# AdaLN block with attention and a mixture of experts: loop instructions re-spread, last value product by token halves, epsilon and relus on other engines, output order at both ends of the experts

## The chip, the cores and the metric

The kernel runs on one core of a Trainium2 chip. The metric is the device time of one execution in microseconds, the median of three runs. The core has a matrix engine (TensorE, PE in the profile), VectorE (DVE), ScalarE (ACT) and GpSimd (POOL), and SyncE (SP), which only issues transfers here. Each runs its own queue of instructions in order, and they wait for each other on semaphores that the kernel sets by hand.

## The reference, cut to what matters

Eight batches of 512 tokens of width 128 go through two layers:

```python
h = layernorm(x) * (1 + ca) + sa                # ca, sa, ga, cb, sb, gb come from silu(c) @ wmod
q, k, v = einsum('bsx,xAnh->Abnsh', h, w)       # 16 heads of 64
q = q + q_bias
a = q @ k.T / 8 + relative_causal(q @ emb.T / 8)
x = x + ga * (softmax(mask(a)) @ v @ out_kernel + out_bias)
h = layernorm(x) * (1 + cb) + sb
score = softmax(h @ Wg + bg); gate = max(score); idx = argmax(score)
# expert e takes its first 256 tokens in order, others give 0
y = relu(buf @ W1[e] + b1[e]) @ W2[e] + b2[e]   # 16 experts, hidden 512
x = x + gb * y[idx, pos] * gate
```

## The kernel before

Layouts put features on partitions for the projections and tokens on partitions for the softmax. To keep float32 accuracy with the fast matrix format, an operand is split in a high part, rounded by a copy on ScalarE (`vhi`, `qhi`, `khi`, `ohi`, `w1hi`, `xhi`), and a low part, the difference (`vlo`, `qlo`, `klo`, `olo`, `w1lo`, `xlo`); a product is then three products: high by high, low by high, high by low. The relative term is folded into the scores: 64 more rows of the contraction hold sines and cosines, so that one score product gives both terms.

**The attention loop** has 64 steps `j`, one for each pair of heads `a` (0 to 7) of each batch `b`. Each step has eight slots `k`; slot `k` makes the scores of head `k // 4` for one block of 128 queries, longest row first (512, 384, 256, 128 keys). Each engine's `step` function writes its order out by hand. On TensorE (L988 on) a slot issues `scores(j, k)` (L878, L875 for the block of 128), and between the slots the transposes of the probabilities of step j-1 (L888, slots 0 to 5, six groups), the value projection for a later step (L864, slot 1), the output product of step j-2 (L915, slot 2), the query projection of head 0 of step j+1 (L843, slot 4, behind the scores), the key projection of step j+1 (L843, slot 5), the product of probabilities and values of step j-1 (L908, slot 7), and behind slot 7 the query projection of head 1. Two banks of PSUM take the scores in turn, so scores `k` wait for the reduction `k-2`.

VectorE reduces each score block with mask and maximum (L1257), makes `qx` from the projected queries (`evac_q`, L1274), the low parts `klo` (`low_k`, L1280) and `olo` (L1286), one group of transposed probabilities in slot 0 (L1265) and the reciprocals of the sums. In slot 4 the order is: reduction, reciprocal, `evac_q` of head 0. ScalarE takes the exponent of each block (`exps`, L623), copies five of the six transposed groups (`evac_pt`, L632; group 4 behind the exponent of slot 4, group 5 before that of slot 5), and makes the high parts. GpSimd makes `qlo` (L451) and divides the probabilities by the sums (L458, four pieces a head).

Around this, two chains per batch are spread over the slots by `before_attention` (statistics, normalisation, `vhi` and `vlo` of the next batch) and `after_attention` (residual, second layer norm, gate logits, choice of the expert, place in the expert's buffer, for the batch before). For the latter TensorE has extra work in given slots: `turn_a` (L923) at step 1, `logits_t` (L944) at step 3 slot 5, `turn_l` (L951) at step 4, `places` (L963 on) at step 5. GpSimd scatters the finished rows (first-layer output, normalised row, gate times its factor, token number) into a buffer in HBM, `xbuf`, sorted by expert.

**Between loop and experts** there is only the last batch. `weighted` (L908) makes the last value product into one bank, `evac_o` and `low_o` split it, `project_out` (L915) adds it to the output, `residual` (L1295) forms the new x in `h2T`, `turn_a_halves` (L931) transposes it for the statistics (L1176), GpSimd adds epsilon (L372) and takes the power -0.5 (L374), and normalisation, gating and placing follow on small tiles. `fill_in` (L1068) issues products whose result nobody reads.

**The experts** go two tiles of 128 slots at a time. For expert `e`: the input, transposed by TensorE (`turn_e`, L1121; for the first three, a sum of the rows already in `xbuf` and a one-hot product for the last batch, L1088 to L1106), is split by ScalarE (`high_x`, L759) and VectorE (`low_x`, L1597); `hidden` (L1130) makes four tiles of 128 hidden units; relu of tiles 0 to 2 is on ScalarE (L768), of tile 3 on VectorE (L1603); `down` (L1143) makes the output; `output` on VectorE adds the bias, multiplies with the gate and adds x (L1618 to L1621); GpSimd scatters the rows to the result (L513). VectorE also makes the low weights (`low_w1`, L1574). Up to expert 9 the output of expert e-1 is made in round e, then two in one round, from then on that of expert e. SP loads rows of the experts (L286 all columns, L297 the columns behind the first 128 for the first three) and weights (L278, L282); `down` of expert e waits until the output e-2 is written.

## Time and profile before

| | |
|---|---|
| median of 3 runs | 883.32 us (882.67 to 883.62) |
| the profiled execution | 884.27 us |
| span from its first to its last instruction | 882.5 us |
| mean granted TensorE clock | 0.995 |
| busy share of the span: TensorE, VectorE, ScalarE, GpSimd | 98%, 75%, 81%, 60% |
| share of the chain that ended last: TensorE, VectorE | 88%, 2% |

The share of busy time is a mean over stages. The loop ends near 788 us, the experts start near 812, and the last scatter is issued near 874. Matmuls overlap, so the duration of one in a row is longer than the distance to the next; what one costs in a stream is read from the distance of the starts.

### The profile page before, as it was taken

What the parts mean: (1) busy time and instruction counts of PE and PEld (TensorE: products, weight loads), DVE (VectorE), ACT (ScalarE), POOL (GpSimd) and SP (SyncE); (2) the same over time, 40 slices, a digit from 0 to 9 for tenths busy, and PEclk for the clock granted to TensorE, in tenths of its full rate; (3) what the DMA queues carried; (4) which work ended last, traced back from release to release, by engine and by line L of the source; (5) the groups of instructions that cost most, each with busy time, mean ns of one, the idle gap of its engine ahead of it and who ended that gap; (6) DMA issues with size and microseconds to landing.
All of it is one profiled execution on the core that took longest, in us unless ns stands there. A gap on an engine that the chain in (4) does not pass through costs nothing.

```text
span 882.5 us, 17635 instructions
## 1 busy us (share of the span) xinstructions
PE 862.1 (98%) x5579; PEld 687.6 (78%) x5579; DVE 664.7 (75%) x2054; ACT 716.4 (81%) x1996; POOL 532.6 (60%) x796
## 2 busy tenths in 40 slices
PE   8999999999999999999999999999999999999995
PEld 7778877778877778777787777787777877777994
DVE  5878777787878687776878677877778677866684
ACT  5888888888888888888988888888888888874562
POOL 3655566576566765676566765676656646673364
PEclk9999999999999999999999999999999999999998
DMA  8000970000000000000000000000000000015870
GB/s 290 2 1 1 259 197 13 13 19 19 13 13 2 36 1 13 13 19 18 13 13 12 16 13 13 1 21 1 14 13 12 11 13 13 2 34 188 282 225 23
DMA packets 25469, 41.42 MB, mean 47 GB/s; under 512 B 3318, under 2 KB 17511, under 8 KB 24992
## 3 DMA queue, kind: packets, MB, share of 16 engines
q1 hardware_dynamic: 21728, 33.60, 12.6%
q0 software_dynamic: 3072, 5.94, 1.9%
q8 instruction: 45, 0.74, 0.4%
q10 hardware_dynamic: 576, 0.75, 0.3%
q14 instruction: 48, 0.39, 0.1%
HBM read 25.93 MB, written 16.82 MB: 48 GB/s over the span
## 4 chain that ended last, share of the span: by engine, by line
PE 88%; DVE 2%; POOL 1%; DMA 1%; issue 1%; ACT 0%; SPq 0%; POOLq 0%; DVEq 0%
PE bank L878 22%; PE bank L843 16%; PE bank L908 16%; PE bank L888 15%; PE bank L915 5%; PE bank L864 4%; PE bank L875 3%; PE bank L1143 2%; PE bank L1130 2%; DMA x<-xbuf 1%; POOL prob L458 0%; ACT prob L623 0%; PE bank L923 0%; POOL out L513 0%; PE bank L826 0%
## 5 line engine op out<-in xcount | busy, mean ns | idle before, releaser
L458 POOL TENSOR_SCALAR prob<-prob,rsum 128x128 f32<-128x128 f32 (+3 forms) x512 | 263.9, 533 | 220.6 <-DVE rsum L1269 214.9
L623 ACT ACTIVATE prob<-srow,nmax 128x512 f32<-128x512 f32 (+3 forms) x512 | 286.5, 561 | 64.5 <-DVE nmax L1257 61.3
L1257 DVE CUSTOM_DVE_ANT_0 srow<-bank,consts 128x512 f32<-128x512 f32 (+3 forms) x512 | 247.5, 488 | 85.8 <-issue 63.9
L888 PE MATMUL bank<-consts,prob 128*128 128x128 f32 x1280 | 201.9, 272 | 0.2 <-POOL prob L458 0.2
L888 PEld LDWEIGHTS bank<-consts,prob 128*128 128x128 f32 x1280 | 158.2, 141 | 22.8 <-POOL prob L458 0.5
L451 POOL TENSOR_TENSOR qlo<-qx,qhi 128x384 fp32r<-128x384 f32 x128 | 129.2, 1009 | 49.6 <-ACT qhi L588 48.6
L632 ACT ACTIVATE pt<-bank 128x384 f32<-128x384 f32 x318 | 152.3, 496 | 1.4 <-PE bank L888 1.3
L908 PE MATMUL bank<-pt,v 128*64 128x512 f32 (+3 forms) x1024 | 152.0, 439 | 0.3 <-issue 0.2
L878 PE MATMUL bank<-khi,qhi 128*128 128x512 f32 (+2 forms) x384 | 145.7, 380 | 2.7 <-DVE nmax L1257 1.9
L1274 DVE SCALAR_TENSOR_TENSOR qx<-bank,qbias,consts 128x512 f32<-128x512 f32 x128 | 94.2, 736 | 60.9 <-PE bank L843 60.8
L878 PE MATMUL bank<-khi,qlo 128*128 128x512 f32 (+2 forms) x384 | 130.0, 339 | 0.0
L878 PE MATMUL bank<-klo,qhi 128*128 128x512 f32 (+2 forms) x384 | 129.1, 336 | 0.0
L908 PEld LDWEIGHTS bank<-pt,v 128*64 128x64 f32 x1024 | 68.2, 136 | 76.7 <-issue 59.2
L1280 DVE SCALAR_TENSOR_TENSOR klo<-bank,khi 64x512 fp32r<-64x512 f32 x128 | 87.8, 686 | 18.1 <-ACT kx L583 16.1
L588 ACT ACTIVATE qhi<-qx 128x384 fp32r<-128x384 f32 x128 | 66.7, 521 | 38.8 <-DVE qx L1274 38.1
L623 ACT ACTIVATION_READ_ACCUMULATOR prob<-srow,nmax 128x1 f32 x512 | 97.8, 191 | 0.0
L878 PEld LDWEIGHTS bank<-khi,qhi 128*128 128x128 f32 x384 | 72.4, 189 | 16.9 <-issue 5.9
L843 PE MATMUL bank<-hhi,whi 128*128 128x512 f32 x177 | 81.6, 461 | 0.0
L878 PEld LDWEIGHTS bank<-klo,qhi 128*128 128x128 f32 x384 | 72.8, 190 | 7.6
L582 ACT ACTIVATE khi<-bank 64x512 fp32r<-64x512 f32 x128 | 75.3, 588 | 2.0 <-PE bank L843 0.5
L878 PEld LDWEIGHTS bank<-khi,qlo 128*128 128x128 f32 x384 | 72.2, 188 | 5.5
L843 PE MATMUL bank<-hlo,whi 128*128 128x512 f32 x177 | 70.0, 395 | 0.0
(210 smaller groups left out, 1419.5 us busy)
## 6 DMA issues: line engine op xcount, KB each, us to landing
xbuf<-fill SPq DMA_DIRECT2D x4, 1540.0 KB, 23.4
x<-xbuf SPq DMA_DIRECT2D x13, 385.0 KB, 3.5
raw<-in_w SPq DMA_DIRECT2D x16, 256.0 KB, 8.7
prob<-in_w SPq DMA_DIRECT2D x16, 256.0 KB, 4.7
h2T<-in_xt SPq DMA_DIRECT2D x8, 256.0 KB, 2.7
out<-row SPq DMA_DIRECT2D x8, 256.0 KB, 2.3
x<-in_x SPq DMA_DIRECT2D x1, 1792.0 KB, 13.4
modb<-mod_rows SPq DMA_DIRECT2D x1, 1536.0 KB, 8.9
```

Of the source, the lines that this page charges most:

```text
L451: gp.tensor_tensor(qlo[:, h, :], qx[:, h, P:S], qhi[:, h, :], ALU.subtract).then_inc(s["ql"], 1)
L458: end = gp.tensor_scalar(part, part, rsum[:, par, 4 * h + q:4 * h + q + 1], 1.0, ALU.mult, ALU.mult)
L582: act.activation(khi[0:HD, h, :], prb[0][h * HD:(h + 1) * HD, :], ACT.Copy, scale=C_QKV)
L623: act.activation(prob[:, par, h, QOFF[q]:QOFF[q] + P * (q + 1)], srow[:, k % 4, 0:P * (q + 1)], ACT.Exp, bias=nmax[:, par, k:k + 1], scale ...
L632: act.activation(pt[:, h, KOFF[g]:KOFF[g] + GW[g]], source[:, 0:GW[g]], ACT.Copy)\
L843: last = pe.matmul(out, w[:, a, cols], h, start=(i == 0), stop=(i == 2))
L878: last = pe.matmul(out, a[:, h, (q - 1) * P:q * P], b[:, h, 0:P * (q + 1)], start=(i == 0), stop=(i == 2))
L888: last = pe.transpose(out[:, n * P:(n + 1) * P], prob[:, par, h, QOFF[q] + k * P:QOFF[q] + (k + 1) * P], ident)
L908: last = pe.matmul(otb[h * HD:(h + 1) * HD, k * P:S], v[:, g, k, at + h * HD:at + (h + 1) * HD], pt[:, h, KOFF[k]:KOFF[k] + S - k * P], st ...
L1257: dve.tensor_tensor_reduce(out=srow[:, k % 4, 0:w], in0=scb[k % 2][:, 0:w], in1=mask[:, S - w:S], scale=-1.0, scalar=BIG, op0=ALU.add, op1 ...
L1274: dve.scalar_tensor_tensor(qx[:, h, :], prb[h][:, :], qbias[:, h, a:a + 1], qtab, ALU.add, ALU.mult).then_inc(s["qe"], 1)
L1280: dve.scalar_tensor_tensor(klo[0:HD, h, :], prb[0][h * HD:(h + 1) * HD, :], C_QKV, khi[0:HD, h, :], ALU.mult, ALU.subtract).then_inc(s["kl ...
```

## The change

It moves instructions and waits, and in two places splits one in two.

- In a step, TensorE projects head 0's queries of step j+1 ahead of score product 4 instead of behind it (not in the first and the last step of the loop), VectorE makes `qx` of it ahead of the reduction of slot 4, and ScalarE copies group 4 ahead of the exponent of slot 4.
- `low` (vlo of the next batch) goes from VectorE, step 4 slot 7, to GpSimd, step 4, ahead of the first division.
- `logits_t` goes from step 3 slot 5 to slot 7, its copy from slot 6 to slot 7. `limits` loses the token numbers, which go to step 3 slot 5, and moves from step 5 slot 3 to slot 5.
- Epsilon of the first batch's first norm and of the last batch's second is added on VectorE.
- The last value product, its split, the last output product and the last residual are done by halves of the tokens in two banks.
- The first hidden layer orders its twelve products so that those with `xhi` come first. All four relus are on ScalarE. The outputs of expert 14 are written by halves in round 15's place, its second half in bank 0. SP issues the other columns of the first experts before the rows of experts 3 and 4.

```diff
 SP
             for e in range(EARLY, NSLOT):
+                other_columns(e - EARLY)
                 rows(e)
-                other_columns(e - EARLY)
 GpSimd
-            def root(i, n):
-                waits(gp, ("pch", 1), (f"rst{i + 1}", n))
-                gp.tensor_scalar(vare[:, i, :], mom[:, i, :, 1], EPS, None, ALU.add).then_inc(s[f"va{i + 1}"], 1)
+            def root(i, n, added=False):
+                gp.wait_ge(s["pch"], 1)
+                if not added:
+                    gp.wait_ge(s[f"rst{i + 1}"], n)
+                    gp.tensor_scalar(vare[:, i, :], mom[:, i, :, 1], EPS, None, ALU.add).then_inc(s[f"va{i + 1}"], 1)
...
+            def low(n):
+                gp.wait_ge(s["vhi"], n + 1)
+                gp.tensor_tensor(vlo[:, :], hn[:, :], vhi[:, :], ALU.subtract).then_inc(s["vlo"], 1)
...
+                    if not last and a == 4:
+                        low(b + 1)
                     divide(j, a % 2, 0)
...
-            root(1, B)
+            root(1, B, True)
 ScalarE
-                    if before and k == 5:
-                        evac_pt(j - 1, 5)
+                    if before and k in (4, 5):
+                        evac_pt(j - 1, k)
                     exps(j, par, k)
...
-                    if before and 2 <= k < 5:
+                    if before and k in (2, 3):
                         evac_pt(j - 1, k)
...
-            evac_o(NJ - 1)
+            for i in range(2):
+                half = slice(i * S // 2, (i + 1) * S // 2)
+                act.wait_ge(s["pv"], NJ + i)
+                act.activation(ohi[:, half], half_o[i][:, half], ACT.Copy, scale=C_QKV * C_OUT).then_inc(s["oe"], 1)
...
-                    for n in range(NB - 1):
+                    for n in range(NB):
                         act.wait_ge(s["hm"], NB * e + n + 1)
 TensorE
                 for k in range(8):
+                    if k == 4 and a == 3 and first:
+                        pe.wait_ge(s["whi"], 8)
+                        pe.wait_ge(s["wlo"], 4)
+                        pe.wait_ge(s["wlo_k"], 2)
+                    if k == 4 and before and after:
+                        project_q(j + 1, n, m, 0)
                     scores(j, k)
...
-                    if (a, k) in ((1, 5), (3, 5), (4, 4), (5, 4)) and not first:
+                    if (a, k) in ((1, 5), (3, 7), (4, 4), (5, 4)) and not first:
...
-            weighted(NJ - 1, PAIRS - 1, NJ, 3)
-            fill_in(6)
-            project_out(NJ - 1, PAIRS - 1)
...
+            for i in range(2):
+                for k in range(2 * i + 2):
+                    c0_, c1_ = max(k * P, i * S // 2), (i + 1) * S // 2
+                    for h in range(2):
+                        at = (PAIRS - 1) % 4 * P + h * HD
+                        last = pe.matmul(half_o[i][h * HD:(h + 1) * HD, c0_:c1_],
+                                         v[:, (PAIRS - 1) // 4, k, at:at + HD],
+                                         pt[:, h, KOFF[k] + c0_ - k * P:KOFF[k] + c1_ - k * P],
+                                         start=(k == 0), stop=(k == 2 * i + 1))
+                last.then_inc(s["pv"], 1)
             fill_in(4)
+            for i in range(2):
+                half = slice(i * S // 2, (i + 1) * S // 2)
+                pe.wait_ge(s["ol"], NJ + i)
+                for n, (w, o) in enumerate(((wohi, ohi), (wohi, olo), (wolo, ohi))):
+                    end = pe.matmul(opb[:, half], w[:, PAIRS - 1, :], o[:, half], start=False, stop=(i == 1 and n == 2))
+            end.then_inc(s["op"], 1)
+            fill_in(2)
             turn_a_halves()
...
+            def hidden_first():
+                pe.wait_ge(s["w1l"], 1)
+                pe.wait_ge(s["xt"], 1)
+                for n in range(NB):
+                    for i, w in enumerate((w1hi, w1lo)):
+                        pe.matmul(bank[2 + n][:, 0:CAP], w[:, 0, n, :], xhi[:, 0, :], start=(i == 0), stop=False)
+                pe.wait_ge(s["xl"], 1)
+                for n in range(NB):
+                    pe.matmul(bank[2 + n][:, 0:CAP], w1hi[:, 0, n, :], xlo[:, 0, :], start=False, stop=True)\
+                        .then_inc(s["hm"], 1)
 VectorE
                 for k in range(8):
+                    if k == 4 and before and after:
+                        evac_q(j + 1, (a + 1) % PAIRS, 0)
                     scores(j, par, k)
...
-                if (a, k) == (4, 7):
-                    low(n)
-                if (a, k) == (3, 6):
+                if (a, k) == (3, 5):
+                    token_numbers(b)
+                if (a, k) == (3, 7):
                     logits_out(b)
...
-                if (a, k) == (5, 3):
-                    limits(b)
                 if (a, k) == (5, 5):
                     place(b)
+                    limits(b)
...
             aggregate(1, B)
+            add_eps(1, B)
...
-                relu(e, e % 2)
...
-                if e >= LAGGING:
+                if LAGGING <= e < E - 2:
                     output(e)
-            relu(E - 1, 1)
+            for t in range(ST):
+                output(E - 2, t, t + 1)
             for t in range(ST):
                 output(E - 1, t, t + 1)
```

## Rows read from the trace of the kernel before

**Rows 1.** Windows, one batch: length, busy time by engine, clock, DMA share, GB/s

```profile
175.40:272.50 97.10, 97.03 (x610) 76.21 (x610) 75.39 (x237) 83.84 (x237) 62.07 (x95) 1.00 0.04 15
```

**Rows 2.** Timeline of TensorE, a step: start us, us, engine, line, operation, count

```profile
204.12 0.47 PE L878 MATMUL bank<-khi,qhi 128*128 128x512 f32 x1
...
204.90 0.40 PE L843 MATMUL bank<-hhi,whi 128*128 128x512 f32 x1
...
205.59 0.49 PE L888 MATMUL bank<-consts,prob 128*128 128x128 f32 x3
```

**Rows 3.** Timeline of VectorE and ScalarE, the same step

```profile
205.19 0.69 DVE L1257 CUSTOM_DVE_ANT_0 srow<-bank,consts 128x512 f32<-128x512 f32 x1 [0.90 <-issue]
...
206.65 0.85 ACT L632 ACTIVATE pt<-bank 128x384 f32<-128x384 f32 x2
```

**Rows 4.** Timeline, end of step 4, step 5, and step 0 of the next batch

```profile
173.80 0.68 DVE L1206 TENSOR_TENSOR vlo<-hn,vhi 128x512 fp32r<-128x512 f32 x1
...
175.18 0.47 PE L878 MATMUL bank<-khi,qhi 128*128 128x512 f32 x1
...
180.29 1.04 POOL L436 TENSOR_TENSOR row<-rsm,modb 128x512 f32<-128x512 f32 x1 [1.37 <-DVE rsm L1362]
...
180.33 1.03 DVE L1376 TENSOR_SCALAR rsm<-rsm 128x4 f32<-128x4 f32 x1
...
183.03 0.50 PE L843 MATMUL bank<-hhi,whi 128*128 128x512 f32 x1
...
218.61 0.50 PE L843 MATMUL bank<-hhi,whi 128*128 128x512 f32 x1
```

**Rows 5.** Timeline of ScalarE and TensorE, a step 2

```profile
243.82 0.49 ACT L632 ACTIVATE pt<-bank 128x384 f32<-128x384 f32 x1
...
244.60 2.38 PE L908 MATMUL bank<-pt,v 128*64 128x512 f32 x16
```

**Rows 6.** Timeline of TensorE, logits of step 3

```profile
255.15 0.43 PE L944 MATMUL bank<-h2T,wgc 128*32 128x128 f32 x8
```

**Rows 7.** Timeline of GpSimd, step 4

```profile
264.08 1.19 POOL L418 TENSOR_TENSOR row<-row,modb 128x512 f32<-128x512 f32 x1
```

**Rows 8.** Timeline of TensorE, first and last batch, fifth score product

```profile
59.22 0.47 PE L878 MATMUL bank<-khi,qhi 128*128 128x512 f32 x1 [0.69 <-DVE nmax L1257]
...
774.01 0.47 PE L878 MATMUL bank<-khi,qhi 128*128 128x512 f32 x1
```

**Rows 9.** Timeline, between the loop and the experts

```profile
800.01 0.75 DVE L1295 SCALAR_TENSOR_TENSOR h2T<-bank,modT,h2T 128x512 f32<-128x512 f32 x1 [0.56 <-PE bank L915]
...
802.75 0.54 POOL L372 TENSOR_SCALAR vare<-mom 128x4 f32<-128x4 f32 x1 [9.65 <-DVE mom L1181]
...
803.37 1.04 POOL L374 TENSOR_TENSOR rstd<-vare,mhalf 128x4 f32<-128x4 f32 x1
...
811.47 0.42 DVE L1597 TENSOR_TENSOR hlo<-bank,hhi 128x256 fp32r<-128x256 f32 x1 [1.11 <-ACT hhi L759]
```

**Rows 10.** DMA issues at 817 (KB, us to landing), timeline of the experts

```profile
x<-xbuf SPq DMA_DIRECT2D x1, 385.0 KB, 3.2
x<-xbuf SPq DMA_DIRECT2D x1, 257.0 KB, 5.0
...
812.04 0.36 PE L1130 MATMUL bank<-hhi,whi 128*128 128x256 f32 x1 [0.33 <-DVE hlo L1597]
...
822.32 0.17 DVE L1615 CAST yidx<-x 128x2 uint32<-128x2 f32 x1 [2.22 <-DMA x<-xbuf]
...
823.86 2.38 PE L1143 MATMUL bank<-prob,srow 128*128 128x128 f32 x16 [1.21 <-DVE row L1621]
...
853.16 1.38 PE L1143 MATMUL bank<-prob,srow 128*128 128x128 f32 x10 [0.62 <-DVE srow L1603]
...
871.67 0.29 DVE L1618 TENSOR_TENSOR xh<-bank,v 128x128 f32<-128x128 f32 x1
...
874.40 0.97 POOL L513 DMA_INDIRECT out<-xh,yidx  x1 [0.30 <-issue]
```

## Prediction of the time after the change

> **What bounds the kernel now.** I read the table of windows first. One batch of attention (64 steps in all, 8 to a batch) takes 97.10 us, TensorE is busy in 97.03 of them at a granted clock of 1.00, which is the 2.4 GHz level, while VectorE, ScalarE and GpSimd rest for 14 to 35 us [rows 1]. So in the loop an edit is worth what it takes out of TensorE's stream, and the other engines matter only where their lateness opens a hole in it. "Busy" hides small holes, since the ends of matmuls are modelled; I found them by comparing start times in the timeline of TensorE: three products of 512 columns follow each other every 0.23 us, and the first behind fp32 transposes costs 0.08 more (204.12 to 204.90 is 0.78) [rows 2]. Measured against that, three holes recur in each batch [rows 4]. Behind the loop the chain alternates between engines, and there the waits at the ends of rows are the prices [rows 8, 9].
>
> **The loop, part by part.** Nothing is added to or taken from TensorE's work in a step; things change places.
>
> Low half of the next batch's activations (`low`), from VectorE to GpSimd. The 0.68 us at 173.80 stands directly before the low half of the keys, and the next step's first score product starts at 175.18, some 0.22 late [rows 4]. The instruction leaves VectorE, so this hole goes: six batches have it, 6 x 0.22 = 1.3 us. On GpSimd a 128x512 operation of two inputs took 1.19 us [rows 7]; it sits in step 4 behind two of those, before the division. The division of the first head must wait for VectorE's reciprocal anyway, and by the timeline it would be ready about 0.5 us later than now, so GpSimd ends at nearly the same time as that reciprocal. Cover: GpSimd's wait. Without it the 1.2 us would push the low half of the queries that the next step's first score needs, up to 0.5 us per batch. I take 0.
>
> Key projection of step 5. It waits for VectorE's qx, which in step 5 comes behind `limits`: 1.03 us at 180.33 for 512 numbers, ending with the GpSimd operation at 180.29 [rows 4]. TensorE's projection at 183.03 starts 0.21 late; in step 0 the same thing happens behind statistics, 0.095 late at 218.61 [rows 4]. Now the projection of the first head's queries goes ahead of score product 4, and qx ahead of that score's reduction, and `limits` and the token numbers leave the place. qx is then ready about 0.7 us sooner, more than either hole: 7 x 0.21 + 7 x 0.095 = 2.1 us. The projection's new wait, for the low half of the keys, ends some 0.6 us before TensorE gets there.
>
> What this swap makes late. The score's reduction, at 205.19 now, follows a product that ends 0.7 us later; the exponent behind it moves by as much. ScalarE fills part of it by copying transposed group 4 first (that group starts at 205.59 on TensorE in either order). The two copies, now one at 206.65 and ending at 207.50 [rows 3], would end about 0.33 later, at 207.83. The weighted product needs them at 208.14 (the start of the same product is at 244.60 in the step below), so an ordinary step has 0.2 us left after the hop between engines. Cost 0. In step 2 ScalarE has a 0.77 us normalisation between the two: the last copy ran from 243.82 to 244.31, the product started at 244.60 [rows 5]; 0.25 later plus a hop of 0.1 is a hole of about 0.07. Seven batches: 0.5 us lost. Bounds 0 and 7 x 0.3 = 2.1.
>
> Transposed logits from slot 5 to slot 7 of step 3. They are eight short matmul records of width 32 from 255.15 to 255.50 [rows 6]. In front of them and behind them TensorE pauses about 0.23 each, and again about 0.24 between the full-width and the 64-wide product of slot 7. Placed there, one of the three changes of width is shared. If a change from 32 to 64 costs what the others do, 0.17 us per batch, 1.2 in all; bounds 0 and 1.2; I take 1.0. SP loads the next transposed input only behind these logits, so that load starts 2 us later; it is wanted in the next batch, some 50 us on. The Trainium skill (TensorEngine Tiling (Array Packing), the section with the rule that mode switching requires a drain) says that changing the tiling mode empties the engine. The pauses at 255.15 agree. By that rule one drain per batch goes, by a reading in which they belong to the logits alone none would.
>
> Ends of the loop. At 59.22 the fifth score of a step of the first batch waited 0.87 us in total (0.69 of it shown) for a late reduction [rows 8]; the projection now fills half of it: 0.4. In the last batch no values are projected, TensorE runs ahead, and the fifth score product waits 0.31 us (start at 774.01) [rows 8]; in two of three such steps the projection now goes in: 0.6. Epsilon on VectorE at the very start saves one hop, 0.15 (bounds 0, 0.35).
> Loop and start: 1.3 + 2.1 - 0.5 + 1.0 + 0.4 + 0.6 + 0.15 = 5.05 us.
>
> **The stretch between loop and experts.** The last value product is made by token halves (384 and 896 of the 1280 columns, so the same total). ScalarE's copy and VectorE's low part of the first half lie beside the second half's product; of the second half only half-wide ones stay on the path. A VectorE operation took 0.75 at 512 columns and 0.42 at 256 [rows 9], so the two save about 0.25 + 0.3, the output product's last part and its shorter end 0.3; the residual in two halves costs 0.15 more, and the first half's transposes and statistics run beside the second: 0.15. Sum 0.85 (bounds 0.4 and 1.3). Epsilon: GpSimd's addition at 802.75 took 0.54, the root started at 803.37, 0.62 after it [rows 9]. On VectorE such a 4-column operation comes without the first hop: 0.4 saved. GpSimd is idle there (9.65 us), and the 0.66 us low part of a weight stands behind the addition in VectorE's order. The Trainium skill (SBUF — State Buffer, "SBUF: two separate sides") says that VectorE in a two-port mode and GpSimd lock each other out for a whole instruction. The pair at 180.29 and 180.33 agrees; the rule speaks against more such operations on VectorE while GpSimd works, and by it `limits`, now beside the divisions, can wait for one of their pieces. That delays a reduction with over a microsecond of slack and leaves the sum as it is. Together 1.25 us; what follows up to the first expert moves with it.
>
> **The experts.** The first hidden layer may start before xlo: 812.04 shows 0.33 of waiting [rows 10], worth up to 0.45. I give it 0, since the chain is then held by a transfer (next).
> Order of loads: rows of expert 3 (385 KB) are issued first and land 3.2 us later, the other columns of expert 0 (257 KB) second, 5.0 us [rows 10]. VectorE waits 2.22 us for the latter until 822.32; its output frees TensorE at 823.86, and the relu on VectorE behind it stretches that product further, until about 826.0. Swapped, the columns land near 819.9 and the output is ready at about 821.4, before TensorE wants it (822.5). Expert 3's rows now come second, near 822.2, and TensorE wants them at 822.3 or a little sooner: the new end of the wait. The second product then runs 822.55 to 824.25. Gain 1.75 us; bounds 0.45 (only the relu part) and 2.1.
> Expert 10: two outputs in a row on VectorE held its relu, TensorE waited to 853.16 (0.62 shown, 0.89 in the spacing of the experts) [rows 10]. Four relus on ScalarE take this away; but the low part of the next input still stands behind both outputs and comes 0.14 late: 0.75 gained. In an ordinary expert ScalarE's queue has 2.6 of 3.43 us filled, and the low part is ready 0.15 before TensorE asks for it: nothing.
> End: four scatters follow each other at 1.27 us on GpSimd, the last at 874.40, while the first half of the last expert's rows is written at 871.7 [rows 10]. With expert 14 written by halves its two scatters go about a microsecond sooner and no longer hold up expert 15's. Those then start behind their own data, the first 0.9 after it (the hop from VectorE to a scatter in the timeline), the last 1.27 later, near 873.9: 0.5 gained (bounds 0, 0.6).
> Experts: 3.0 us.
>
> **Sum.** 5.05 + 1.25 + 3.0 = 9.3 us. The profiled execution took 884.27 us around a span of 882.5, so this one would take 875.0. It lies 0.95 above the median of the runs, 883.32; from that the forecast is **874.0 us**.
>
> **Rivals.**
> A. The holes of the loop move instead of going: a later reduction or copy (step 2, the root of step 2 on GpSimd before the low queries) takes back what the three holes give. For it: slacks of 0.1 to 0.3 us; against it: each is still positive by rows. The loop then gives about 1.5 instead of 5: 877.6.
> B. The swapped transfers do not help, since the rows of expert 3 land late, and the halves gain nothing because of more instructions: the tail gives 1.7 instead of 4.25: 876.6.
> C. Slower. ScalarE decides: its copy of group 5 ends past the time of the weighted product in every step. It happens from 0.2 us more than I count; at 0.4 us more each of some 55 steps loses 0.2, 11 us, against gains of 9.3: 885.0. For it: ScalarE's queue is unbroken from 203.4 to 211.4 in a step; against it: it then rests 0.8 us, so the lateness doesn't add up from step to step.
> D. It doesn't do what it says: score product 4 is so late that TensorE itself waits and nothing is won in the loop, and the tail is as in B: 881.5.
>
> **Chances.** Forecast 0.60, A 0.20, B 0.12, C 0.04, D 0.04. A measurement here tells 0.2%, 1.8 us, from no change. All but C and part of D are faster: faster 0.94, same 0.02, slower 0.04. Range: the forecast's own bounds are 871.5 to 876; A and B reach to 878.5. I give 871.5 to 878.5.
>
> **What would show it.** Right: a batch of 96.4 or 96.5 us instead of 97.1; VectorE's qx at 0.5 before the key projection; weight product 0.23 after the projection at the end of step 4; about 0.1 of waiting before the weighted product in step 2. The root some 1.25 us sooner after the last value product; no wait of TensorE before expert 2's output product, and a short one before expert 3's transposes; experts 3.43 us apart at expert 10. Wrong: a new recurring wait for ScalarE's copies or GpSimd's low queries, or batches of 97 us and more.

## The result and the profile after

The changed kernel takes **869.92 us** (median of 4 runs, 868.92 to 871.30), the kernel before 883.47 us (882.67 to 883.91): ratio 0.9849, 95% interval 0.9832 to 0.9866. The forecast was 874.0 us with a range from 871.5: the sign was right, the gain of 13.5 us is 4.2 more than the 9.3 that the sum gave, and the time lies below the range.

The profiled execution took 869.76 us around a span of 867.7. The head of its page (busy us, share of the span, instructions of each engine; below it the chain's shares):

```profile
PE 851.8 (98%) x5586; PEld 685.2 (79%) x5586; DVE 657.8 (76%) x2038; ACT 726.3 (84%) x2013; POOL 541.9 (62%) x801
...
PE 92%; ACT 1%; DVE 1%; POOL 1%; issue 1%; POOLq 0%; DVEq 0%
```

TensorE's share of the span is 98% in both kernels, and its share of the chain rose from 88% to 92%. One batch in the windows view, the row that answers to [rows 1] (its bounds are the starts of two weighted products eight steps apart):

```profile
209.53:305.29 95.76, 95.76 (x611) 75.92 (x611) 75.42 (x236) 84.70 (x237) 63.28 (x96) 1.00 0.05 15
```

A batch takes about 95.8 us instead of 97.1; the forecast was 96.4 or 96.5. The granted clock is 1.00 in both, the upper level. The start of the weighted product is a good ruler, one per step and every step with the same work around it. I list its distance from step to step in both traces (us); a row belongs to the step that the distance ends in:

| stretch | before | after | difference |
|---|---|---|---|
| an ordinary step (6, 7 of a batch) | 11.82 | 11.75 | -0.07 |
| step 0 | 11.94 | 11.75, once 11.82 | -0.19 |
| steps 1 and 2 | 12.26 | 12.19 | -0.07 |
| step 3 | 12.38 | 12.10 to 12.12 | -0.27 |
| step 4 | 11.94 | 11.89 to 11.91 | -0.03 |
| step 5 | 12.65 | 12.03 to 12.07, in one batch 12.34 | -0.6, once -0.3 |
| first to last weighted product | 757.06 | 746.75 | -10.3 |
| from there to the end | 87.4 | 82.9 | -4.5 |

The tail gave 4.5 where the forecast had 4.25. The loop gave 10.3 where it had 5.05, and the 0.07 of nearly every step is most of what is missing. (The first and the last batch differ in some steps; they are told below.)

**Where the 0.07 was.** The same place of a step in the kernel before, VectorE and TensorE (start us, us, engine, line, operation):

```profile
312.42 0.42 DVE L1257 CUSTOM_DVE_ANT_0 srow<-bank,consts 128x256 f32<-128x256 f32 x1
312.58 0.60 PE L888 MATMUL bank<-consts,prob 128*128 128x128 f32 x4
312.77 0.08 DVE L1257 DVE_READ_ACCUMULATOR2_ANT nmax<- 128x1 f32 x1
...
313.00 0.47 PE L878 MATMUL bank<-khi,qhi 128*128 128x512 f32 x1
```

and after:

```profile
309.07 0.60 PE L903 MATMUL bank<-consts,prob 128*128 128x128 f32 x4
309.43 0.48 PE L854 MATMUL bank<-hhi,whi 128*128 128x512 f32 x1
...
310.21 0.39 PE L893 MATMUL bank<-khi,qhi 128*128 128x512 f32 x1
```

The four transposes of slot 3 are followed by the next product 0.42 later before (312.58 to 313.00) and 0.36 later after (309.07 to 309.43). Before, that product was score product 4, and it starts 0.15 behind the end of VectorE's reduction of slot 2 (312.77 + 0.08 = 312.85), which frees its bank. The same 0.15 stands at 59.22 and 774.01 [rows 8], where I had read the wait, and at 204.12 [rows 2], where I had not, since it is too short there for the profile to name a releaser. In all 63 steps of the kernel before in which such a product follows transposes, the distance is 0.14 or 0.15. Now the query projection is at that place and covers it.

**The holes of [rows 4]** are gone, with two exceptions. TensorE in the second batch after: last product of the queries and first score product of step 5, last transposes and key projection of step 5.

```profile
173.35 0.39 PE L854 MATMUL bank<-hhi,wlo 128*128 128x512 f32 x1
173.58 0.39 PE L893 MATMUL bank<-khi,qhi 128*128 128x512 f32 x1
...
180.83 0.49 PE L903 MATMUL bank<-consts,prob 128*128 128x128 f32 x3
181.07 0.48 PE L854 MATMUL bank<-hhi,whi 128*128 128x512 f32 x1
```

The distances are 0.23 and 0.24, those of an unbroken stream. In the sixth batch a hole stays in front of the first score product of step 5, and the step is 0.3 longer than in the others:

```profile
554.09 1.00 POOL L459 TENSOR_TENSOR qlo<-qx,qhi 128x384 fp32r<-128x384 f32 x1
554.32 0.86 DVE L1423 SCALAR_TENSOR_TENSOR lgt<-lgt,consts 128x64 f32<-128x64 f32 x1
...
555.83 0.68 DVE L1335 SCALAR_TENSOR_TENSOR klo<-bank,khi 64x512 fp32r<-64x512 f32 x1
...
556.61 0.47 PE L893 MATMUL bank<-khi,qhi 128*128 128x512 f32 x1
```

There VectorE's reduction of slot 5 came 0.35 later than in the other batches (nothing in the profile says why), so that other small operations of the gate chain lay beside GpSimd's work: the one at 554.32 took 0.86 instead of 0.40 and ended 0.09 behind GpSimd's `qlo`. `klo`, which follows, ended 0.57 later than elsewhere, and the score product started 0.10 behind it. The same hole, 0.3 and in the same batch, stands in the traces of the kernels t2_late, t02_late and power_alone below. The other exception is step 0 of the fourth batch, where 0.07 of the 0.12 stays.

### The profile page after: what moved, and what is told of

Same layout as the page of the kernel before. It is cut to its first block, busy times and chain, and to the rows that moved or that the text cites. A ratio compares the mean times of both kernels' runs of the same rounds, so it can differ in the third digit from the quotient of the medians.

```text
span 867.7 us, 17644 instructions
## 1 busy us (share of the span) xinstructions
PE 851.8 (98%) x5586; PEld 685.2 (79%) x5586; DVE 657.8 (76%) x2038; ACT 726.3 (84%) x2013; POOL 541.9 (62%) x801
## 4 chain that ended last, share of the span: by engine, by line
PE 92%; ACT 1%; DVE 1%; POOL 1%; issue 1%; POOLq 0%; DVEq 0%
PE bank L893 22%; PE bank L923 16%; PE bank L854 16%; PE bank L903 16%; PE bank L930 5%; PE bank L878 5%; PE bank L890 3%; PE bank L1189 3%; PE bank L1164 2%; ACT prob L633 1%; POOL prob L466 0%; PE bank L938 0%; PE bank L837 0%; PE bank L1084 0%; POOL out L523 0%
## 5 line engine op out<-in xcount | busy, mean ns | idle before, releaser
L642 ACT ACTIVATE pt<-bank 128x384 f32<-128x384 f32 x318 | 157.0, 498 | 11.1 <-PE bank L903 11.0
L923 PE MATMUL bank<-pt,v 128*64 128x512 f32 x1008 | 149.6, 439 | 0.2
L893 PE MATMUL bank<-khi,qhi 128*128 128x512 f32 (+2 forms) x384 | 140.4, 366 | 0.6 <-DVE nmax L1312 0.4
L854 PE MATMUL bank<-hhi,whi 128*128 128x512 f32 x177 | 85.8, 485 | 0.0
```

The source lines that it names most:

```text
L642: act.activation(pt[:, h, KOFF[g]:KOFF[g] + GW[g]], source[:, 0:GW[g]], ACT.Copy)\
L854: last = pe.matmul(out, w[:, a, cols], h, start=(i == 0), stop=(i == 2))
L893: last = pe.matmul(out, a[:, h, (q - 1) * P:q * P], b[:, h, 0:P * (q + 1)], start=(i == 0), stop=(i == 2))
L923: last = pe.matmul(otb[h * HD:(h + 1) * HD, k * P:S], v[:, g, k, at + h * HD:at + (h + 1) * HD], pt[:, h, KOFF[k]:KOFF[k] + S - k * P], st ...
```

## Experiments

All twelve were timed beside the kernel before. I give ratios to it, since its own time was not always the same (886.94 beside the first four kernels, 883.47 and 883.13 beside the others). Where the ruler of weighted products says more, I give it too; over the whole loop it varied by 0.3 us between the five kernels, that of before among them, that leave the loop as it is or move only a wait.

**The swap in slot 4 alone.** TensorE, VectorE and ScalarE as in the change's diff, with TensorE's waits moved to fit; its main lines:

```diff
+                    if k == 4 and before and after:
+                        project_q(j + 1, n, m, 0)
                     scores(j, k)
```

> The kernel before with one part of the change alone: in slot 4 TensorE projects head 0's queries ahead of score product 4, VectorE makes qx ahead of that slot's reduction, ScalarE copies group 4 ahead of the exponent. Theory (cover): before, the fifth score product waited in every step for VectorE's reduction of slot 2, which frees its bank; it starts 0.15 us after that reduction's end and 0.07 later than its stream allows. With the projection ahead the wait is hidden: 62 steps x 0.07 = 4.4, with the holes of the key projection 7 x 0.21 + 7 x 0.095 = 2.1 (less if limits, still in its old place, holds qx), 0.5 in the first and 1.1 in the last batch: 7.5 to 8.3 us, 875 to 876. Rival (the forecast's own sum: an ordinary step gains nothing, step 2 loses 0.5): 2.1 - 0.5 + 0.4 + 0.6 = 2.6, 880.9.

Measured 0.9923 (0.9908 to 0.9939), 6.8 us; by the ruler 6.8. Every ordinary step went from 11.82 to 11.75, step 0 from 11.94 to 11.75, step 5 from 12.65 to between 12.39 and 12.44. Beyond that the swap gave 0.4 in step 3 of the first batch and 0.66 in steps 5 to 7 of the last, whose step 3 lost 0.27 of it. In that batch no values are projected, the swap brings TensorE to step 3 sooner still, and its first score product now waits for GpSimd's low queries, which stand behind the root of step 2; the changed kernel shows the same:

```profile
722.68 1.00 POOL L459 TENSOR_TENSOR qlo<-qx,qhi 128x384 fp32r<-128x384 f32 x1
723.73 0.19 PEld L893 LDWEIGHTS bank<-khi,qhi 128*128 128x128 f32 x1 [0.43 <-POOL qlo L459]
```

The forecast's own 2.6 is refuted. The cover theory's 7.5 came 0.7 short, by that loss, by step 5, where qx still had `limits` in front of it, and by step 3 of the third batch, 0.13 longer than in the others for no reason that I know.

**Only the wait moved.**

```diff
                     pe.wait_ge(s["ql"], 2 * j + h + 1)
-                    pe.wait_ge(s["kl"], 2 * j + h + 1)
+                    if k == 0 or j in (0, NJ - 1):
+                        pe.wait_ge(s["kl"], 2 * j + h + 1)
...
+                    if k == 3 and before and after:
+                        pe.wait_ge(s["kl"], 2 * j + 2)
```

> The kernel before, with nothing moved but one wait of TensorE: the wait for the low half of the keys, which stood directly ahead of score product 4 beside those for the low queries and the bank, stands ahead of slot 3's transposes. Cover theory: the bank's wait decides, so nothing changes: 883.4 within 0.5, ordinary steps 11.82. Rival (waits): the fifth score product pays 0.07 for having three waits in front instead of two, and the change took one away: 62 x 0.07 = 4.4 sooner, 879.0, steps of 11.75.

Measured 0.9997 (0.9988 to 1.0007); ordinary steps of 11.81 to 11.84. Fewer waits in front of the product give nothing.

**VectorE's reduction earlier, TensorE untouched.**

```diff
                     if k == KLO:
-                        low_k(j, 1)
+                        low_k(j, 1, S if first or last else S // 2)
```

> The kernel before with VectorE's low half of the second head's keys, which stands in slot 1 ahead of the reduction of slot 2, made for 256 of its 512 columns in batches 2 to 7 (the other columns keep old values; the kernel leaves this work out). The reduction of slot 2 then ends some 0.27 us sooner and TensorE's order and waits are those of before. Cover theory: the fifth score product starts 0.07 sooner in each of these 48 steps, 3.4 us in all, and the key projection of steps 5 and 0 may gain up to 0.1 to 0.2 as well, since qx follows sooner: 878.5 to 880. Rival (waits, or a fixed cost of that place in TensorE's order): nothing but that last part, 0 to 2 us: 881.5 to 883.4, ordinary steps still 11.82.

Measured 0.9947 (0.9934 to 0.9960), 4.7 us. In batches 2 to 7 an ordinary step is 11.76, in the first and the last, where nothing was shortened, still 11.82. The same place of the step in its trace:

```profile
310.16 0.43 DVE L1257 CUSTOM_DVE_ANT_0 srow<-bank,consts 128x256 f32<-128x256 f32 x1
...
310.51 0.08 DVE L1257 DVE_READ_ACCUMULATOR2_ANT nmax<- 128x1 f32 x1
...
310.58 0.60 PE L888 MATMUL bank<-consts,prob 128*128 128x128 f32 x4
...
310.94 0.47 PE L878 MATMUL bank<-khi,qhi 128*128 128x512 f32 x1
```

TensorE has the order of the kernel before and score product 4 comes 0.36 behind the transposes, as the projection does in the changed kernel. So the wait for slot 2's reduction is shown from both sides: covering it or ending it sooner gives the same 0.07. Step 5 gained 0.32 here, more than I expected, as qx came sooner too.

**Logits alone:**

```diff
-                    if (a, k) in ((1, 5), (3, 5), (4, 4), (5, 4)) and not first:
+                    if (a, k) in ((1, 5), (3, 7), (4, 4), (5, 4)) and not first:
```

> The kernel before with the logits of step 3 moved from slot 5 to slot 7 on TensorE, their copy on VectorE from slot 6 to slot 7, and nothing else. Forecast on record: one change of width saved, 0.17 a batch, 1.0 to 1.2 us. Reading of the two traces: step 3 is 0.20 shorter than its share of the other gains, 7 x 0.20 = 1.4: 882.0. Rival: the 0.20 comes from another part (the swap in slot 4), and the logits alone give nothing: 883.4.

Measured 0.9979 (0.9968 to 0.9990), 1.9 us; by the ruler 1.44, all of it in step 3, 12.38 to between 12.17 and 12.19 in seven batches. Forecast 1.0. In their old place the logits started 0.42 behind the three transposes (254.73 to 255.15), where a product starts 0.24 behind them, and the key projection's first product took 0.34 to its successor instead of 0.32: 0.20, which is what went.

**VectorE relieved in steps 3 to 5:**

```diff
 GpSimd
+                    if not last and a == 4:
+                        low(b + 1)
 VectorE
-                if (a, k) == (4, 7):
-                    low(n)
-                if (a, k) == (5, 3):
-                    limits(b)
...
                     place(b)
+                    limits(b)
```

> The kernel before with VectorE relieved in steps 3 to 5 and TensorE's order untouched: low (vlo of the next batch) on GpSimd in step 4, limits from step 5 slot 3 to slot 5, the token numbers in step 3 slot 5. Forecast on record: 6 x 0.22 for low; the key projection's hole of step 5 was put down to limits, so 7 x 0.21 for it: 1.3 + 1.5 = 2.8 us, 0.32 percent of the time; no new wait for GpSimd's low queries. In the trace the step that ends at step 5's weighted product is 0.4 shorter, all others equal to 0.02. Rival (the hole of step 5 belongs to the order of slot 4, not to limits): 1.3 us only, 0.22 in that step. Rival A of the record (GpSimd late, holes move): nothing in sum, the step behind longer.

Measured 0.9967 (0.9956 to 0.9979), 2.9 us; by the ruler 3.3: step 5 went from 12.65 to 12.10 in six batches and by 0.24 in the last; all others are equal to 0.03 but for one, step 0 of the fourth batch, which took 0.35 more (VectorE waited for a late exponent there once, and TensorE for its qx). So both holes went, 0.1 more with them, and no step got longer in every batch. The 0.1 is this: a product behind a hole also reaches its successor later, 0.30 (175.18 to 175.48) instead of 0.23 (175.18 to 175.41 in this run's trace). A hole of 0.22 so costs 0.3.

In sum by the ruler: 6.8 + 1.44 + 3.3 = 11.6. The change as a whole gave 10.3: swap and relief both take from step 5. In batches 2 to 7 they gave 1.4 and 3.3 there alone and 3.3 together (0.3 of it lost to the sixth batch's hole), so 1.4 is counted twice. That closes to 0.1, though single steps that took 0.1 to 0.35 longer once, as above, are in these sums too.

**Between loop and experts alone:** the change's diff from `weighted(NJ - 1` to `fill_in(2)`, with its parts on ScalarE and VectorE, and `add_eps(1, B)`.

> The kernel before with the stretch between loop and experts changed alone: last value product, its split, last output product and residual by token halves, and the last batch's epsilon on VectorE. Forecast on record: 0.85 + 0.4 = 1.25 us. Reading of the two traces, from the start of the last value product: the root starts 1.26 sooner (8.27 to 7.01), but its power takes 1.34 instead of 1.04 beside a VectorE operation, so that the mean behind it comes 0.96 sooner. So 0.95 to 1.0 at the mean and at the first hidden product; the loop's steps all equal. Rival (halves cost more instructions than they save): below 0.5.

Measured 0.9992 (0.9984 to 1.0001), which the times alone do not tell from no change; in the profile the tail from the start of the last value product is 86.4 instead of 87.4 and all steps are equal to 0.03, so 1.0.

**The experts alone:** the change's diff of SP, from `hidden_first` on, and of the relus.

> The kernel before with the experts' part changed alone: first hidden layer's order, four relus on ScalarE, order of SP's first loads, expert 14 by halves. Forecast on record 3.0 us (load order and relu 1.75, expert 10 0.75, end 0.5, first hidden layer 0). Reading of the traces: 67.4 instead of 70.5 from the first hidden product to the end, 3.1, and some 0.4 more in which the first hidden product comes sooner: 3.4 to 3.5. Rival B of the record (the swapped transfers do not help since expert 3's rows land late): 1.3 to 1.7.

Measured 0.9962 (0.9949 to 0.9975), 3.4 us; the tail 83.9 instead of 87.4. First hidden product 0.46 sooner, 3.1 from there to the end.

**The order of SP's loads alone:**

```diff
             for e in range(EARLY, NSLOT):
+                other_columns(e - EARLY)
                 rows(e)
-                other_columns(e - EARLY)
```

> The kernel before with one thing changed: SP issues the other columns of the first experts' rows before the rows of experts 3 and 4. Forecast on record: VectorE's wait of 2.22 us for the columns of expert 0 shrinks to 0 or nearly, and expert 2's output product starts at once; with the relu still on VectorE 1.3 of the 1.75 us come, since that relu (0.45) still stands behind an output. Rival B (expert 3's rows, now second, land at least as late as the columns did and hold TensorE instead): 0 to 0.5.

Measured 0.9980 (0.9971 to 0.9988), 1.8 us; the tail 85.6, 1.8 less. From the first hidden product to expert 2's output product 10.47 instead of 11.82, then 0.4 more, since the relu is no longer late either. VectorE and TensorE where [rows 10] had 2.22 and 1.21 of waiting:

```profile
822.11 0.17 DVE L1615 CAST yidx<-x 128x2 uint32<-128x2 f32 x1 [0.40 <-DMA x<-xbuf]
...
824.09 1.95 PE L1143 MATMUL bank<-prob,srow 128*128 128x128 f32 x16
```

**Could more be had in the loop?** The first product behind transposes starts its successor 0.31 later instead of 0.23, at six places of a step. I tried to merge such places.

```diff
-                    if before and k in TURN:
+                    if before and k in TURN and k != 2:
...
                         project_out(j - 2, (a - 2) % PAIRS)
+                    if before and k == 2:
+                        transposes(j - 1, 1 - par, 0, 2)
```

> The changed kernel (0.9849 of before) with one more move: in slot 2 TensorE makes transposes 2 behind the output product of step j-2 instead of ahead of it, so that they stand next to the fp32 score product and the transposes of slot 3. Theory (transition): the first product behind fp32 transposes costs 0.08 more wherever it stands; here one such place per step goes, 61 steps x 0.08 = 5 us: 865, ratio 0.979, ordinary steps 11.67 instead of 11.75. Rival (the 0.08 is the price of the transposes and stays with them, or the fp32 score product behind them pays it): no change, 870, steps 11.75. Rival (the copy of group 2 on ScalarE, 0.2 to 0.4 later, delays score product or copies behind): steps longer than 11.75.

Measured 0.9867 (0.9852 to 0.9882), no gain on the changed kernel's 0.9849; by the ruler its loop is even 2.2 longer. Slot 2 and 3 of its TensorE:

```profile
308.19 0.41 PE L930 MATMUL bank<-ohi,wohi 128*128 128x512 f32 x1
308.44 0.39 PE L930 MATMUL bank<-olo,wohi 128*128 128x512 f32 x1
...
308.90 0.49 PE L903 MATMUL bank<-consts,prob 128*128 128x128 f32 x3
309.22 0.39 PE L890 MATMUL bank<-kx,qx 128*128 128x128 f32 x2
```

The output product lost its 0.06 to 0.08 (0.25 to its successor), but the three transposes are now followed by the fp32 score product after 0.32, where three transposes before a product take 0.25 (307.82 to 308.07 in the changed kernel). So the price went with leaving transposes here too, with another kind of product behind them, and nothing is saved.

```diff
-                    if before and k in TURN and k != 2:
+                    if before and k in TURN and k not in (0, 2):
+                        if k == 1:
+                            transposes(j - 1, 1 - par, 0, 0)
```

> As the kernel with late transposes 2, and transposes 0 also moved, behind the second score product, next to transposes 1. Theory (transition): two places per step less than in the changed kernel: 61 x 0.16 = 10 us: 860, ratio 0.973, steps 11.59. VectorE's copy of group 0 comes behind its first reduction in any case and has 0.1 us of slack. Rival (that copy or ScalarE's copy of group 1 becomes late): the second move gives nothing, 865. Rival (no transition cost): 870.

Measured 1.0040 (1.0027 to 1.0054): slower than before, steps of 12.02. The seven transposes took 0.68 (310.71 to 311.39), no less than 0.36 + 0.25 apart, so joining two groups of transposes isn't free either. The loss is a new wait: VectorE's copy of group 0 moved back, the low part of the output behind it as well, and TensorE waits for that:

```profile
299.33 0.69 DVE L1324 COPY pt<-bank 128x512 f32<-128x512 f32 x1 [0.16 <-PE bank L903]
...
299.94 0.68 DVE L1345 SCALAR_TENSOR_TENSOR olo<-bank,ohi 128x512 fp32r<-128x512 f32 x1
...
300.67 0.19 PEld L930 LDWEIGHTS bank<-ohi,wohi 128*128 128x128 f32 x1 [0.22 <-DVE olo L1345]
```

```diff
-                    if before and k in TURN and k not in (0, 2):
-                        if k == 1:
-                            transposes(j - 1, 1 - par, 0, 0)
+                    if before and k in TURN and k not in (0, 2, 4):
+                        if k in (1, 5):
+                            transposes(j - 1, 1 - par, *divmod(k - 1, 3))
```

> As the kernel with late transposes 0 and 2, and transposes 4 also moved, behind the sixth score product, next to transposes 5; ScalarE copies both groups ahead of the fifth exponent, which comes some 0.6 us later for it. Theory (transition): three places per step less: 61 x 0.24 = 15 us: 855, ratio 0.968, steps 11.5. Rival (ScalarE decides: the later exponent pushes qhi and with it the low queries that the next step's first score product waits for): the third move costs more than its 0.08, 860 to 866, with a wait of TensorE at the first score product or at the weighted product.

Measured 1.0064 (1.0051 to 1.0078), steps of 12.02 again. The theory on which these three rested, that putting groups of transposes next to other fp32 work saves 0.08 each, has fallen.

**GpSimd's power with VectorE quiet beside it.**

```diff
             add_eps(1, B)
-            low_w1(1, 1)
...
                 if e == 0:
-                    for q in range(QT):
+                    low_w1(1, 1)
+                    for q in range(3):
                         one_of(2, q)
```

> The changed kernel with one VectorE operation moved away from beside GpSimd's power in the stretch behind the loop: the low part of expert 1's weight, 128x512, goes from directly behind the addition of epsilon to behind the low rows, with one of the one-hot tiles behind it. Theory (the two engines disturb each other): the power takes 1.04 instead of 1.34 and the mean behind it comes 0.3 sooner, some 0.3 us of the total, which the times cannot tell. Rival (the power's length has another cause): 1.34 again. Nothing else changes.

Measured 0.9835 (0.9820 to 0.9850), the fastest of all, but not told from the changed kernel by the interval; its tail is 82.6 instead of 82.9, and the other 1.1 of its shorter span lies ahead of the first weighted product, which this edit does not touch. The power, in the changed kernel:

```profile
791.51 0.17 DVE L1236 TENSOR_SCALAR vare<-mom 128x4 f32<-128x4 f32 x1
791.59 0.68 DVE L1648 TENSOR_TENSOR wlo<-raw,whi 128x512 fp32r<-128x512 f32 x1
791.83 1.34 POOL L377 TENSOR_TENSOR rstd<-vare,mhalf 128x4 f32<-128x4 f32 x1 [9.00 <-DVE vare L1236]
```

and in this one:

```profile
790.27 0.17 DVE L1236 TENSOR_SCALAR vare<-mom 128x4 f32<-128x4 f32 x1
790.35 0.16 DVE L1463 COPY row<-consts 128x4 f32<-128x4 f32 x1
790.59 1.04 POOL L377 TENSOR_TENSOR rstd<-vare,mhalf 128x4 f32<-128x4 f32 x1 [8.99 <-DVE vare L1236]
```

1.34 beside the 128x512 operation, 1.04 without it: 0.44 of VectorE's operation was left when the power started (791.59 + 0.68 - 791.83), and the power lost 0.30. The section of the Trainium skill named in the forecast (SBUF — State Buffer, "SBUF: two separate sides") also counts VectorE operations with two inputs in SBUF, as this one has, beside a GpSimd operation that reads SBUF: the later of the two waits. The trace agrees in kind; the loss is 0.14 less than what was left. In the kernel before the same operation lay beside GpSimd's addition, whose 0.54 [rows 9] is long for four columns (the median of its line's 16 is 0.24); the change moved the collision from the addition to the power.

## Why the forecast was wrong, point by point

- **The failed step: "so an ordinary step has 0.2 us left after the hop between engines. Cost 0."** The cost was 0, but the wait in front of score product 4 was put at nothing, without a look: 0.07 in each of 62 steps, 4.3 us with the swap alone (in the whole change step 4 gave only 0.03 in six batches, and why is open), about the whole miss. I judged score product 4 by the distance of the starts behind it (204.12 to 204.90, [rows 2]); the excess there is the price of transposes and stays. The hole stood in front of it, between the transposes and its start. Three holes per batch were searched for against a typical step; a hole that is in every step is part of the typical step and can't be found so.
- `low`, 1.3, and the key projection, 2.1: the two moves on VectorE gave 3.3 without the swap, where 1.3 + 1.5 had been counted; the swap alone takes 0.12 more than its 0.07 at step 0, where 0.095 had been counted. In each case the hole was read rightly, and the slower successor behind it was left out.
- Loss in step 2, 0.5: it did not come. Step 2 gained the same 0.07 as others. In the trace after, the last copy there runs from 337.33 to 337.80 and the weighted product starts at 337.90, in its stream: 0.10 is enough for the hop, and the copy came 0.19 later than before against this product (0.29 ahead of it before [rows 5]), not the 0.25 that was counted.
- Logits 1.0: right in direction, 1.44 in size, above its upper bound of 1.2, since 0.20 a batch went where 0.17 had been taken (of the pauses of 0.23 that were read in front of the logits and behind them, 0.18 and 0.02 belonged to their place). By the rule of the Trainium skill on draining at a change of tiling mode, cited in the forecast, one drain goes; the trace agrees with that, but no run changed the width alone, without the place.
- First batch 0.4: 0.4. Last batch 0.6: 0.66 by the swap in steps 5 to 7, less the 0.27 in step 3, where TensorE waits for GpSimd's low queries (rival A had named this, behind the root of step 2). Epsilon at the start 0.15: nothing to be seen, the first weighted product is at 38.05 before and 38.07 after, and it lies anywhere from 36.9 to 39.8 in the other traces.
- Between loop and experts 1.25: 1.0. The root starts 1.26 sooner as said; its power then takes 0.3 longer beside VectorE, which the forecast had not priced, though it cited the rule on the shared ports for `limits`, where nothing depended on it.
- Experts 3.0: 3.4 to 3.5. Load order and relu 1.75: 1.8, already with the relu on VectorE. Expert 10: 0.9, all of its 0.89 and not the 0.75 counted; the output products are 3.42 apart from 841.80 to 845.22. The end: 0.6 for 0.5; of expert 15's two scatters only the last still queues behind another:

```profile
858.39 0.97 POOL L523 DMA_INDIRECT out<-xh,yidx  x1 [0.66 <-issue]
859.67 0.97 POOL L523 DMA_INDIRECT out<-xh,yidx  x1 [0.30 <-issue]
```

  The first hidden layer, put at 0 "since the chain is then held by a transfer", started 0.46 sooner, its upper bound, and 0.3 of that is left at expert 0's output product (2.60 behind the first hidden product instead of 2.43) and behind: the load order had removed that transfer from the chain. Two edits of one change had been judged against different kernels. (No run has the new order of the first layer without the new load order; this is argued from the rows.) So the tail's 4.5 against 4.25 is a sum of misses: -0.25 between loop and experts, +0.5 in the experts.
- Rivals A to D all said less gain. Of A, holes that move, two came, 0.27 and 0.3 us, once each. None had a gain in the ordinary step, and the range, built from them, was open only on that side. "Wrong: a new recurring wait" did not occur, and for a batch shorter than 96.4 the list had no line.

## What to carry to other kernels

Before costing a reorder of a pipelined loop, take one ordinary step and check at every product whether its start follows its predecessor or the engine that frees its bank: a start at a constant small distance behind another engine's end, in every step, is a wait, though the profile names none. Then swap in work that needs nothing. When several edits act on one chain, cost each with the others applied; and put no long VectorE operation with both inputs in SBUF beside GpSimd's link of a serial chain.

## What the runs showed of the hardware that was not expected

- TensorE started 0.15 us behind the end of the VectorE instruction that released it (the read of the reduction's accumulator), at 59.22, 313.00 and 774.01, and with the wait for the keys moved away 0.15 again. Behind VectorE's `klo` it was 0.10 (step 5 of the kernel before).
- A product behind a hole of 0.1 to 0.2 us also reached its successor up to 0.07 later (0.30 instead of 0.23 at 175.18), so that the hole cost more than its width.
- VectorE's operation on the gate scores that ran beside GpSimd's `qlo` in step 4 ended 0.07 to 0.09 us behind the end of `qlo`, in the seven batches that have it, in each of seven traces (before, after, loop_order, low_limits, t2_late, t02_late, power_alone): 0.75 to 0.87 long, where the same operations took about 0.22 without GpSimd beside them.
- Leaving transposes cost 0.07 to 0.08 with a rounded product behind them (0.31 to its successor instead of 0.23) and with an fp32 one (0.32 instead of 0.25), and the seven transposes joined took 0.07 more than four and three apart.
- The logits put next to the 64-wide product, which saves one of three changes of width, were worth 0.20 us.
- A step that a build does not touch repeated to 0.05 us, but for a single one in some traces (0.35 in low_limits), while the first weighted product started between 36.9 and 39.8, and in the first four runs the tail, untouched there, took 89.5 to 90.3 us instead of 87.4.
